# Closing the stages without GpSimd's drain, and summing the last stage's rows in PSUM

## The reference, cut to what matters

```
x = _layernorm(x + _L0_attn_ref(x, ...))
x = _layernorm(x + _L0_ffn_ref(x, ...))
x = _layernorm(x + _L1_attn_ref(x, ...))
x = _layernorm(x + _L1_ffn_ref(x, ...))

# in _L1_ffn_ref
topv, topi = jax.lax.top_k(gates, TOP_K)            # TOP_K = 2
probs = jax.nn.softmax(topv, axis=-1)
comb = jnp.einsum('nke,nk->ne', jax.nn.one_hot(topi, E, dtype=xf.dtype), probs)
h = gelu(jnp.einsum('nd,edh->enh', xf, w1) + b1[:, None, :])
y = jnp.einsum('enh,ehd->end', h, w2) + b2[:, None, :]
moe_out = jnp.einsum('ne,end->nd', comb, y)
return (shared_out + moe_out).reshape(B, L, D)
```

## Time and profile before

| | us |
|---|---|
| median of 3 runs | 1634.45 (1633.99 to 1639.09) |
| the profiled execution's own time | 1633.04 |
| its span, first to last instruction | 1631.2 |
| `attention0` closes (GpSimd's drain L193 starts) | 669.2 |
| `routed0` closes (L746) | 895.8 |
| `attention1` closes (L1232; barrier at 1435.0) | 1424.6 |
| `routed1` closes (L973) | 1578.9 |
| the last stage's first load is issued | 1585.59 |

### The profile page before, as it was taken

The page is one execution under the profiler, slowest core; times in us unless marked ns, Lnnn a source line. Parts: engine busy times, 40 slices in busy tenths (PEclk is TensorE's granted clock), DMA queues, the critical chain, the costliest instruction groups (busy, mean ns, idle before and its releaser), DMA issues. The chain is left out here.

```text
span 1631.2 us, 35670 instructions
## 1 busy us (share of the span) xinstructions
PE 1392.3 (85%) x10839; PEld 1132.1 (69%) x10840; DVE 1077.9 (66%) x3450; ACT 895.7 (55%) x2391; POOL 647.9 (40%) x978
## 2 busy tenths in 40 slices
PE   5999999999999998299998269999999998988840
PEld 4777777777777777188887157777777776778740
DVE  4777777777777776266665358888888874833326
ACT  3656666666666665055554136777666766832213
POOL 1344444444444444133333232344445333325542
PEclk9999999999999999599999559999999999999975
DMA  6112020202020200011111621022214000023214
GB/s 219 52 36 72 20 73 19 73 19 73 19 73 19 74 22 13 21 42 47 48 46 38 215 67 53 30 73 73 74 47 150 7 15 15 14 67 83 79 59 126
DMA packets 59992, 96.36 MB, mean 59 GB/s; under 512 B 11140, under 2 KB 49412, under 8 KB 57432
## 3 DMA queue, kind: packets, MB, share of 16 engines
q1 hardware_dynamic: 50632, 76.47, 15.3%
q0 software_dynamic: 8864, 18.43, 3.3%
q10 hardware_dynamic: 432, 0.66, 0.1%
HBM read 75.01 MB, written 61.60 MB: 84 GB/s over the span
## 5 line engine op out<-in xcount | busy, mean ns | idle before, releaser
L362 POOL TENSOR_TENSOR a_prob<-a_prob,a_rl 128x128 f32<-128x128 f32 (+1 forms) x258 | 125.5, 508 | 256.1 <-DVE a_rl L447 255.8
L250 ACT ACTIVATE a_prob<-psum,a_nmx 128x128 f32<-128x128 f32 (+1 forms) x516 | 212.3, 423 | 11.9 <-DVE a_nmx L442 11.9
L1989 DVE TENSOR_REDUCE a_mx<-psum 128x2 f32<-128x512 f32 x256 | 170.8, 689 | 41.8 <-PE psum L1320 38.1
L276 ACT ACTIVATE a_probt<-psum 128x768 f32<-128x768 f32 x128 | 103.9, 811 | 118.9 <-PE psum L639 118.9
L1680 ACT ACTIVATE a_prob<-psum 128x1024 f32<-128x1024 f32 x128 | 129.2, 1025 | 13.8 <-PE psum L1352 13.2
L441 DVE TENSOR_REDUCE a_nmx<-psum 128x2 f32<-128x256 f32 x130 | 55.2, 425 | 118.1 <-PE psum L592 118.1
L771 POOL DMA_INDIRECT yt<-m_yrow,m_dest x71 | 67.9, 956 | 158.6 <-DVE m_yrow L922 157.5
L639 PE MATMUL psum<-ident,a_prob 128*128 128x128 f32 x768 | 106.3, 275 | 14.0 <-DVE a_prob L451 14.0
L1320 PE MATMUL psum<-a_k_stk,q_stk 128*128 128x256 f32 x512 | 109.5, 312 | 3.1 <-DVE a_mx L1989 2.1
L288 ACT ACTIVATE a_ot<-psum,a_bias 128x256 f32<-128x256 f32 x128 | 61.4, 480 | 88.1 <-PE psum L665 84.2
L250 ACT ACTIVATION_READ_ACCUMULATOR a_prob<-psum,a_nmx 128x1 f32 x516 | 108.5, 210 | 0.0
(11 more groups left out here) (346 smaller groups left out, 4245.4 us busy)
## 6 DMA issues: line engine op xcount, KB each, us to landing
xs<-in_fill SPq DMA_DIRECT2D x144, 264.0 KB
a_stage<-in_w SPq DMA_DIRECT2D x16, 384.0 KB, 4.3
m_xrow<-xs SPq DMA_DIRECT2D x39, 132.0 KB
m_xrow<-xs SPq DMA_DIRECT2D x71, 66.0 KB, 1.8
a_yin<-yt SPq DMA_DIRECT2D x16, 256.0 KB, 2.8
f_yin<-yt SPq DMA_DIRECT2D x8, 512.0 KB, 4.1
yt<-m_yrow,m_dest POOLq DMA_INDIRECT x149, 2.2
a_xin<-in_x SPq DMA_DIRECT2D x17, 128.0 KB, 2.1
```

Source lines behind the costliest of these rows:

```text
L250: last = nc.scalar.activation(prob[:, slot, h, at], S[:, 2 * slot + h, at], ACT.Exp, bias=nmx[:, slot, q, h:h + 1], accum_out=lsum[:, slot ...
L276: nc.scalar.activation(probt[:, hp % 2], PT[:, :, 0:SW], ACT.Copy).then_inc(pt_done, 1)
L362: last = nc.gpsimd.tensor_tensor(prob[:, slot, 0, at], prob[:, slot, 0, at], rl[:, slot, 0, q:q + 1].to_broadcast(prob[:, slot, 0, at].sha ...
L1989: nc.vector.reduce_max(mx[:, :, h:h + 1], bank.rearrange("p (q k) -> p q k", q=QB), AX.X).then_inc(mx_done, 1)
```

## The change

1. All five blocks are opened with `no_gpsimd_drain=True`, and the two extra barriers with `sem_only=True`: GpSimd's drain ahead of each block's barrier is gone, and so are the drains of the second barriers. The call that clears the semaphores is unchanged, its drain included. The other engines' drains at a block's end stay; each has its count on the barrier in an instruction of its own now.
2. The gates are computed at the start of `routed1` and not of `final1`: tanh on ScalarE, two VectorE instructions.
3. ScalarE makes 64 diagonal matrices of 128x128 (identity times the gate of the row) in `routed1`, two after each of the first 32 blocks, kept in SBUF as `g.diag` (32 KB per partition).
4. In `final1` PE sums in PSUM, one bank per group: the residual times the identity (one matmul of 512 columns), then 8 matmuls of 128 columns, diagonal times expert rows. The first four residuals are issued before any rows arrive, the others behind the experts of group n-4. VectorE's two passes are gone; its statistics and ScalarE's output read PSUM.
5. Stores are issued by ScalarE, each behind a wait for its own output; SP only loads, and a load waits for PE (the slot's sums done) and not for VectorE. GpSimd's power and VectorE's shift wait for ScalarE's output of group n-2.

```diff
@@ the five blocks and the two barriers @@
-    with nc.Block() as block:
+    with nc.Block(no_gpsimd_drain=True) as block:
...
-            nc.all_engine_barrier()
+            nc.all_engine_barrier(sem_only=True)
@@ routed1 @@
+            def diagonals(k):
+                if k == 0:
+                    act.wait_ge(pr_done, 2)
+                for c in range(2):
+                    nc.scalar.activation(g.diag[:, k, c, :], g.ident[:], ACT.Copy, scale=pr[:, c, k:k + 1])
+
+            nc.scalar.activation(th[:], g.gap[:], ACT.Tanh, scale=0.5).then_inc(th_done, 1)
             for j in range(-2, N):
                 if 0 <= j:
                     gate(j)
                 if j + 2 < N:
                     turned(j + 2)
+                if 0 <= j < NTL:
+                    diagonals(j)
@@ final1, SyncE @@
                 if n >= SLOTS:
-                    sp.wait_ge(res_done, n - SLOTS + 1)
+                    sp.wait_ge(sum_ps, n - SLOTS + 1)
...
-            for n in range(SLOTS):
+            for n in range(NG):
                 load(n)
-            for n in range(NG):
-                if n + SLOTS < NG:
-                    load(n + SLOTS)
-                sp.wait_ge(out_done, n + 1)
-                sp.dma_start(d["out"][(n + 1) * GT:(n + 2) * GT].rearrange("(b p) f -> p b f", p=P), out[:, n % 2]
-                             ).then_inc(stored[n % 2], 16)
@@ final1, GpSimd @@
                 pool.wait_ge(var_done, n + 1)
+                if n >= 2:
+                    pool.wait_ge(out_done, n - 1)
@@ final1, TensorE @@
+            def residual(n):
+                nc.tensor.matmul(g.psum[:, n, :], g.ident[:], g.x1[:, n * GT:(n + 1) * GT], start=True, stop=False)
+
+            def experts(n):
+                pe.wait_ge(y_in[n % SLOTS], (n // SLOTS + 1) * 16)
+                for b in range(GB):
+                    for c in range(2):
+                        last = nc.tensor.matmul(g.psum[:, n, b * P:(b + 1) * P], g.diag[:, n * GB + b, c, :],
+                                                yin[:, n % SLOTS, b, c, :], start=False, stop=b == GB - 1 and c == 1)
+                last.then_inc(sum_ps, 1)
+
+            for n in range(SLOTS):
+                residual(n)
+            for n in range(NG):
+                experts(n)
+                if n + SLOTS < NG:
+                    residual(n + SLOTS)
@@ final1, ScalarE @@
-                    last = nc.scalar.activation(out[:, n % 2, b, :], res[:, n % 2, b, :], ACT.Identity,
+                    last = nc.scalar.activation(out[:, n % 2, b, :], g.psum[:, n, b * P:(b + 1) * P], ACT.Identity,
                                                 scale=rstd[:, n % 2, b:b + 1], bias=shift[:, n % 2, b:b + 1])
                 last.then_inc(out_done, 1)
+                act.wait_ge(out_done, n + 1)
+                act.dma_start(d["out"][(n + 1) * GT:(n + 2) * GT].rearrange("(b p) f -> p b f", p=P), out[:, n % 2]
+                              ).then_inc(stored[n % 2], 16)
@@ final1, VectorE @@
-            def residual(n):
-                dve.wait_ge(y_in[n % SLOTS], (n // SLOTS + 1) * 16)
...
+            def variances(n):
+                dve.wait_ge(sum_ps, n + 1)
                 for b in range(GB):
-                    last = nc.vector.bn_stats(stats[:, b, :], res[:, n % 2, b, :])
+                    last = nc.vector.bn_stats(stats[:, b, :], g.psum[:, n, b * P:(b + 1) * P])
...
             def shifts(n):
                 dve.wait_ge(rstd_done, n + 1)
+                if n >= 2:
+                    dve.wait_ge(out_done, n - 1)
```

More of the change, by code:

```diff
@@ L959, in routed1 @@
     yrow = sb("yrow", [P, YSLOTS, 2, P])
+    th, pr = sb("th", [P, NTL]), sb("pr", [P, 2, NTL])
     G, HT, Y, XT = g.psum[:, 0:2, :], g.psum[:, 2:4, :], g.psum[:, 4:6, 0:BR], g.psum[:, 6:8, 0:BR]
@@ L2310, in final1 @@
     out = sb("out", [P, 2, GB, P])
-    th_done, consts, dve_chain, var_done, rstd_done, res_done, shift_done, out_done = (sem(n) for n in (
-        "th_done", "consts", "dve_chain", "var_done", "rstd_done", "res_done", "shift_done", "out_done"))
+    consts, dve_chain, sum_ps, var_done, rstd_done, shift_done, out_done = (sem(n) for n in (
+        "consts", "dve_chain", "sum_ps", "var_done", "rstd_done", "shift_done", "out_done"))
     y_in = [sem(f"y_in{k}") for k in range(SLOTS)]
     stored = [sem("stored0"), sem("stored1")]
-    with nc.Block() as block:
+    with nc.Block(no_gpsimd_drain=True) as block:
         @block.sync
@@ L2341, in _ @@
                 pool.wait_ge(var_done, n + 1)
+                if n >= 2:
+                    pool.wait_ge(out_done, n - 1)
                 nc.gpsimd.tensor_tensor(rstd[:, n % 2, :], veps[:], halfs[:], ALU.pow).then_inc(rstd_done, 1)
+        @block.tensor
+        def _(pe):
+            def residual(n):
[13 more added lines that the diff above has]
+                    residual(n + SLOTS)
         @block.scalar
         def _(act):
-            nc.scalar.activation(th[:], g.gap[:], ACT.Tanh, scale=0.5).then_inc(th_done, 1)
             for n in range(NG):
@@ L2351, in _ @@
                 for b in range(GB):
-                    last = nc.scalar.activation(out[:, n % 2, b, :], res[:, n % 2, b, :], ACT.Identity,
+                    last = nc.scalar.activation(out[:, n % 2, b, :], g.psum[:, n, b * P:(b + 1) * P], ACT.Identity,
                                                 scale=rstd[:, n % 2, b:b + 1], bias=shift[:, n % 2, b:b + 1])
                 last.then_inc(out_done, 1)
+                act.wait_ge(out_done, n + 1)
+                act.dma_start(d["out"][(n + 1) * GT:(n + 2) * GT].rearrange("(b p) f -> p b f", p=P), out[:, n % 2]
+                              ).then_inc(stored[n % 2], 16)
+            for k in range(2):
+                act.wait_ge(stored[k], NG // 2 * 16)
         @block.vector
@@ L2386, in shifts @@
                 dve.wait_ge(rstd_done, n + 1)
+                if n >= 2:
+                    dve.wait_ge(out_done, n - 1)
                 nc.vector.scalar_tensor_tensor(shift[:, n % 2, :], mv[:, n % 2, :, 0], -1.0, rstd[:, n % 2, :], ALU.mult, ALU.mult
                                                ).then_inc(shift_done, 1)
-            dve.wait_ge(th_done, 1)
-            nc.vector.tensor_scalar(pr[:, 0, :], th[:], 0.5, 0.5, ALU.mult, ALU.add)
-            chain.done(nc.vector.tensor_scalar(pr[:, 1, :], th[:], -0.5, 0.5, ALU.mult, ALU.add))
-            residual(0)
+            variances(0)
             for n in range(1, NG):
-                residual(n)
+                variances(n)
                 shifts(n - 1)
@@ L2509, in program @@
         nc.clear_and_free_semaphores(g.sems)
-        nc.all_engine_barrier()
+        nc.all_engine_barrier(sem_only=True)
         g.yt = yt[1]
+        g.diag = keep("diag", [P, NTL, 2, P])
         with ExitStack() as a:
```

22 lines of the change are left out of this document (4 added, 18 removed).

## The result

Over four runs each, the changed kernel takes 1607.48 us (1606.07 to 1611.39) against 1634.22 us (1631.11 to 1639.09): a ratio of 0.9835, 95% interval 0.9811 to 0.9858, or 26.7 us less. The forecast was 11.3 us less. The time lies at the lower end of the range, and 27 us less, 1607, was the price of the second rival, "the drain's time is gone when the drain is".

A forecast was written before the change was run, and what follows sets the result against it. PE was busy 85% of the span, but the change was taken to touch only the seams and last stage. Seams -1.6, diagonals +0.5 and last stage -10.2 gave -11.3 us: 1634.45 to 1623, range 1607 to 1633.

The forecast's parts named there:

- the second rival: At the closings: removed drains' time is gone, L2496 and L2509 stay short; -27 us, 1607 us; chance 0.08.
- What a drain costs: GpSimd's drains: each costs about 0.15 + 0.0805 n us, n being its DMAs since the last drain.
- Which drain meets the work: At the clearing calls: their drains take over open DMAs, 5.3 us at L2496 and 11.0 at L2509.
- The upper end: Clearing drain L2509 after `attention1`: bounds 0 and +10.8 us, of which +10.8 was taken.
- The seam after `routed0`: No clearing call there, so the drain's 5.9 us go: net -5.9 us, 71 DMAs staying open.
- The seam after `routed1`: At the close of `routed1`: the drain's 6.4 us go, net -6.4 us.
- Diagonals: 64 ScalarE activations in `routed1`, two per block taking 0.82 us, mostly hidden: +0.5 us.
- The fourth rival: In `routed1`: diagonals delay the Gelu and hold up PE, up to 26 us, 1648 us; chance 0.09.
- The last stage: `final1` with sums on PE: clock rises at 5 us, stage 35.5 us in place of 45.7, -10.2 us.
- The fifth rival: In the last stage: the clock stays at 1.2 GHz, PE needs 48 us, program 1644 us; chance 0.05.
- The first rival: At L2509: GpSimd clears some work while issuing later DMAs; +5.1 in place of +10.8 us, 1617 us; chance 0.18.
- `attention1`: The stage `attention1` itself: no change in its length, 0 us.

The follow-up runs named there:

- e4: The kernel before with GpSimd's closing drain left out in the block of `routed0` alone; 1608.41 us against 1613.85, ratio 0.9978.
- e2: The changed kernel with the default closings back (GpSimd's drains, full barriers), so diagonals and last stage alone; 1604.12 us against 1613.85, ratio 0.994.
- e5: The kernel before with two plain GpSimd drains in a row in `routed1`, behind the 40th of 78 indirect DMAs; executed once, 1633.35 us.
- e6: The kernel before with an additional 64-row indirect DMA ahead of each of the 71 in `routed0`; executed once, 1680.46 us.
- e10: The kernel before with series of indirect DMAs and drains on GpSimd alone behind its last stage; executed once, 3524.55 us.
- e7: The changed kernel with four slots of `out` in place of two in the last stage and stores issued by SP; 1606.29 us, ratio 0.9811.
- e1: The kernel before with the closings alone changed (five blocks and two barriers without GpSimd's drain); 1596.99 us against 1613.85, ratio 0.9897.

## Why the prediction was wrong, step by step

- **What a drain costs.** Right for a plain drain up to 112 DMAs: 0.15 + 0.0805 n, from four stages, against 0.05 + 0.0816 n in the series.
- **Which drain meets the work.** This is the step that failed: "GpSimd's drain at L2496 about 5.3 us, at the second clearing call about 11 us". It measured 0.137 and 0.176 us: a clearing call's drain takes none of a plain drain's time. That is shown by the changed kernel and by the closings alone. Whether the call settles the work in no time or leaves it alone is not shown. The step cost the sum 5.3 + 10.8 = 16.1 us, and the forecast was off by 15.4.
- **"The upper end".** The bounds for L2509 were 0 and +10.8, and I took the upper because all six drains lie on one line. But the two short ones (n = 0) said nothing about a clearing drain with work before it: no such row existed. I had put two kinds of drain on one line. Even a plain drain would not have read 11.0 there: e4's read 5.87, since 135 is beyond where the line holds.
- **The seam after `routed0`.** Forecast -5.9, measured -5.9.
- **The seam after `routed1`.** Forecast -6.4, measured -4.8. The drain's 6.4 went, but scatters waited in GpSimd's queue when VectorE ended, 1.6 us more than before. On the other chip the pair with and without drains gives -4.9, so it repeats. Nor does it belong to this stage's own drain. Less that drain, the seam is 6.0 us in the traces of the kernel before, e2, e5 and e6, where no earlier drain is left out (6.7 in e10). It is 7.6 to 7.7 in seven where some are, e4 with `routed0`'s alone among them (14.02 - 6.43), and 9.1 in e7. Why is open.
- **Diagonals.** Forecast +0.5, measured +0.7 in the first pair. On one chip `routed1` took 118.9 and 125.1 us with them (the changed kernel, e2), 120.9 and 118.7 without (e1, e4): nothing can be seen. The fourth rival falls; in the first trace PE waited 1.0 us in all for ScalarE's `hid`.
- **The last stage.** Forecast 35.5 us, measured 34.0. The clock rose 5.4 us after PE's start (forecast 5) from 0.50 to 1.00, that is to 2.4 GHz; the first groups took 2.64 (forecast 3.0), the last 1.8 on PE and 2.02 on ScalarE (forecast 2.0 and 2.2). I had not seen ScalarE's wait for the store, 2.90 us. The fifth rival falls. The Trainium skill, "TensorE: Matmul & The Clock Gate", section "What's actually happening", says that activity releases the throttled state. The trace agrees: 0.50 up to 1577.0 and 1.00 from 1577.4, with PE at work without a gap since 1572.0.
- **The rivals.** The second was right, and I gave it 0.08. That its 27 us meet the measured 26.7 so closely is partly luck: its seam of -6.4 came out at -4.8 and the last stage's -10.2 at -11.7, the untouched stages added 1.7 in the traces, and on the other chip the whole change is worth 30.6. The first rival asked for a second clearing drain of some 5.3 us and falls. Its idea, that some of the work is cleared without a drain, holds somewhere beyond 112 DMAs, where it was not needed.
- **`attention1`.** Forecast 0, +4.5 in the first pair. On the chip with four traces it is 528.8 to 529.8 with and without drains. On the slower ones it is 531.8 to 533.8 in three traces with drains and 534.0 to 538.1 in five without. The means are 3.2 us apart, so a loss of some 3 us may be hidden there; it is not settled.

## What to carry to other kernels

A GpSimd drain behind software DMAs is work by itself, some 0.08 us per DMA since the last drain (up to 112 of them here), even when every one has landed; where semaphores already say that the data is there, leaving it out gains what of it lies on the path (here 16.2 us at the seams, of 17.6 that stood there). Before a cost is moved to another instruction, look for a row in which exactly that kind of instruction has met it; two kinds of drain on one fitted line were nearly the whole error here. After a stage is sped up on one engine, look whether the store's landing has become the next wait: with two slots of output it did, for 2.9 us in the trace, though four slots showed no gain in the runs.

## What the runs showed of the hardware

- A plain drain on GpSimd: 0.05 us with nothing open and nothing running (1.12 behind an instruction that still ran for 1.04), 1.36, 3.32, 6.57, 7.88 and 9.18 us after 16, 40, 80, 96 and 112 indirect DMAs of 128 rows; with 64 or 32 rows each the same per DMA.
- After 128, 142 and 200 it took 1.83, 2.98 and 7.71 us: 106 DMAs less than were issued, with no pause among the DMAs.
- The drain in a clearing call: 0.13 to 0.19 us, with none, 64 or 135 DMAs issued since the last plain drain.
- A drain's record can begin before the instruction ahead of it: e5's first began 1.0 us before the 40th DMA and ended 3.3 us after that DMA's end.
- An indirect DMA occupies GpSimd for 0.96 us with 128 rows, 0.90 with 64 and 0.86 with 32, at one per 1.26, 1.20 and 1.17 us.
- One and the same stage, `routed1`, took 118.7 us on one chip and 137 on another.
